# Relation coefficients moved ahead of the fourth softmax piece, with one float32 product per four slots

## The chip, the cores and the metric

The kernel runs on one core of one Trainium2 chip. The metric is the time of one execution in device microseconds. A profiled execution gives the trace, in which every instruction has a start and a duration. PE is TensorE (PEld its weight loads), DVE is VectorE, ACT is ScalarE, POOL is GpSimd and SP is SyncE.

## What is computed

Four layers over N = 3125 nodes with D = 256 features: a graph layer over 50,000 edges, a mixture of experts whose gates come from graph attention, a second graph layer with relations, and a last mixture of experts. The change concerns the seam of the second and the third:

```python
# attention scores: a softmax over the 32768 edges of each target, then
msg = h[src] * alpha[:, :, None]
agg = jax.ops.segment_sum(msg, dst, num_segments=M)
...
# third layer: each edge has one of 32 relations, mixed from 8 bases
weight = jnp.einsum('rb,bio->rio', w_comp, bases)
xw = jnp.einsum('ni,rio->nro', h, weight)
msg = xw[src, rel_type] * norm
out = jax.ops.segment_sum(msg, dst, num_segments=h.shape[0])
```

The kernel does not form `xw`. It uses `w_comp[rel_type] * norm`, eight coefficients for each edge: these are the relation coefficients, `coefs` (tile `slot_coefs`), of 128 partitions by KT = 592 slots by 8 bases. They depend only on the inputs.

## The kernel before

The function `attention_and_experts` writes the program of each engine by hand; the engines meet through semaphores, and each engine runs its own list in order.

*Experts.* Twenty units (4 experts by 5 chunks) run on TensorE as `up` (L1633) and `down` (L1646). ScalarE applies the gelu (L1529), VectorE adds a bias to the results (L1840), and SP stores them.

*Gathers.* Beside the units POOL gathers one row per attention edge into `gall`, 256 gathers of 128 edges (L1487), in 64 groups of four. Before each group it waits until a gather two groups back has landed, and for the progress of the experts that `experts_before(i)` names; groups 57 to 63 wait for the last unit's products only.

*Softmax pieces.* The edges lie in 256 columns that `CUT` divides into four pieces. `piece(c)` on VectorE waits until its columns have landed, scans for the running maximum (L1801), lets ScalarE take the exponents (`exponents`, L1520) and scans for the sums (L1820). The last piece, columns 224 to 256, comes after the last unit. ScalarE's queue stores its sums, and SP loads the rows of the experts' results (L1459) once the last sums are ready.

*Carry and ends.* The sums that run over from one partition to the next are worked out by VectorE, TensorE (L1657 to L1663) and ScalarE (L1538). POOL gathers the sums at the segments' ends, 25 gathers (L1495), and scatters the carry among them (L1494). L1895 on VectorE, which waits for the end gathers, starts the rest of the attention; TensorE combines the experts afterwards (L1692).

*Relation coefficients.* Between the carry and L1895 stands a loop of RS = 37 steps, 16 slots each. In a step VectorE compares the slots' relations with the 32 relations (`relations`, L1880, bf16 one-hots); TensorE turns four blocks of 128 by 128 (`turn_relations`, L1670); ScalarE copies them out of PSUM (L1543); TensorE multiplies each block, as the stationary operand, with the mixing weights of 32 columns (L1683); and VectorE multiplies with the edge's norm into `coefs` (L1891). One-hots, turned blocks and both PSUM banks are double buffered. The weights are float32. So that bf16 products give them in full, VectorE has split them into three bf16 parts (L1769, L1771), and each block is multiplied three times into the same sum.

`coefs` lies where the experts' second weights `W2` are, the one-hots in the first half of the experts' `W1`, and the turned blocks in the second. So the loop can't begin before the last unit.

Of the kernel before, what the change touches and what calls it, by code (L numbers as in the profile page):

```python
# [9 lines left out]
P = 128  # L10
# [1250 lines left out]
GATHERS = 4  # L1261
HALVES = [(kind, m) for m in range(-1, UNITS) for kind, m in (("up", m + 1), ("down", m)) if 0 <= m < UNITS]


def experts_before(i):
# [3 lines left out]
    if half >= len(HALVES):  # L1269
        return HALVES[-1][0], CT * UNITS  # L1270
# [8 lines left out]
def attention_and_experts(nc, common, a, X, iota, ident, att, drams, coefs, y_dram, xn_dram):  # L1279
# [3 lines left out]
    with ExitStack() as ctx:  # L1283
# [29 lines left out]
        relhot_t = [free.bitcast(BF16)[:, k * RQ // QT * P:(k + 1) * RQ // QT * P].rearrange("p (q e) -> p q e", e=P) for k in range(2)]  # L1313
        wparts = sb("wcomp_parts", [P, 3, QT * BASES], BF16)
# [19 lines left out]
        wrest = flags[:, :, :].rearrange("p n w -> p (n w)")[:, 0:QT * BASES]  # L1334
# [133 lines left out]
        def _(pool):  # L1468
# [12 lines left out]
            for i in range(GT // GATHERS):  # L1481
# [3 lines left out]
                pool.wait_ge(h_ready if kind == "up" else y_ready, items)  # L1485
# [12 lines left out]
        def _(act):  # L1498
# [24 lines left out]
            for m in range(UNITS):  # L1523
# [7 lines left out]
                for c in range(PIECES):  # L1531
                    if min(AFTER_UNIT[c] + 2, UNITS - 1) == m:
                        exponents(c)
            act.wait_ge(sums_ready, PIECES)
# [4 lines left out]
            for i in range(RS):  # L1539
                act.wait_ge(relt_ready, i + 1)  # L1540
                if i > 1:
                    act.wait_ge(coef_ready, i - 1)
                nc.scalar.activation(relhot_t[i % 2].rearrange("p q e -> p (q e)"), relt_ps[i % 2], ACT.Copy).then_inc(relt_copied, 1)  # L1543
# [32 lines left out]
        def _(pe):  # L1576
# [79 lines left out]
            pe.wait_ge(carry_steps, ENDS)  # L1656
            nc.tensor.matmul(lines_ps[:, 0, :], sums[:, GT - 1, 0:GW], att.after[:, :], start=True, stop=True)  # L1657
            nc.tensor.matmul(lines_ps[:, 1, :], last_top[:, :], att.after[:, :], start=True, stop=True)
            nc.tensor.matmul(lines_ps[:, 2, :], flags[:, 0, :], ident[:, :], start=True, stop=True)
            nc.tensor.matmul(lines_ps[:, 3, :], flags[:, 1, :], att.after[:, :], start=True, stop=True).then_inc(carry_replies, 1)  # L1660
            pe.wait_ge(carry_steps, RUN)
            nc.tensor.matmul(carry_ps[:, 0:GW], run[:, :], ident[0:GW, 0:GW], start=True, stop=True)
# [34 lines left out]
        def _(dve):  # L1697
# [70 lines left out]
            for n in range(3):  # L1768
                link(V.tensor_copy(wparts[:, n, :], left))  # L1769
                if n < 2:  # L1770
                    link(V.tensor_tensor(wrest, left, wparts[:, n, :], ALU.subtract))  # L1771
                    left = wrest
# [690 lines left out]
```

## Time and profile before

| | |
|---|---|
| runs | 2454.57, 2449.64, 2442.05 us, median 2449.64 |
| profiled execution | 2446.71 us, its span 2444.9 us |
| PE busy | 1714.3 us (70% of the span) |
| DVE busy | 1305.3 us (53%) |
| ACT busy | 701.2 us (29%) |
| POOL busy | 1070.8 us (44%) |
| mean granted TensorE clock | 0.829 |

An engine is busy while it runs an instruction; waits, and the issue of DMAs by SP and ScalarE, are not counted. The granted clock is the share of full speed that TensorE's clock had: 1.00 is 2.4 GHz and 0.50 is 1.2 GHz. In the rows below, [... <-X] is the idle time of the engine just before an instruction, and what ended it as far as the trace shows; "remote" is a semaphore event that it can't place, "issue" no wait that it shows. Times are counted from the start of the span. A group's form is partitions by elements, with the type.

### The profile page before, as it was taken

To read this page: it belongs to the slowest core of one execution; us is meant where nothing else is said; L and a number is where in the kernel's file an instruction comes from. 1 tells how busy PE (TensorE), PEld (TensorE's weight loads), DVE (VectorE), ACT (ScalarE), POOL (GpSimd) and SP (SyncE) were. 2 spreads that over 40 slices of the span, in tenths; PEclk is the share of its full clock that TensorE was granted. 3 is DMA by queue.
4 is the path that set the end of the run, shared out by engine and by line. 5 is a ranking of instruction groups with operands and counts; after the bars stand their busy time and mean duration, and the time that the engine had idled before them with its cause. 6 is when DMAs were issued, how large, how long until landed. Compare 5 with 4: busy or idle time off the path is not lost. (4 is left out here: it accounts for less than half of the span.)

```text
span 2444.9 us, 36227 instructions
## 1 busy us (share of the span) xinstructions
PE 1714.3 (70%) x8780; PEld 1361.2 (56%) x8781; DVE 1305.3 (53%) x3720; ACT 701.2 (29%) x1570; POOL 1070.8 (44%) x1102
## 2 busy tenths in 40 slices
PE   2775567677768999994163556566556667996998
PEld 1443345445446877783153545556545555885776
DVE  7876766677675213122275546556556665225335
ACT  0011255555523222220055322223222221001221
POOL 2676666565514666666402555545554550000000
PEclk9876687887889999997577776777877778998999
DMA  4223233333332232321415333333433332332001
GB/s 161 80 86 95 82 98 100 95 104 100 96 92 14 77 85 85 85 80 51 121 56 182 96 113 103 109 105 112 121 108 105 103 107 106 121 140 65 7 1 53
DMA packets 164850, 226.27 MB, mean 93 GB/s; under 512 B 35636, under 2 KB 123990, under 8 KB 161942
## 3 DMA queue, kind: packets, MB, share of 16 engines
q0 software_dynamic: 47392, 105.58, 15.8%
q1 hardware_dynamic: 114048, 115.99, 15.3%
q10 hardware_dynamic: 3318, 3.59, 0.4%
q8 instruction: 44, 0.72, 0.1%
q14 instruction: 48, 0.39, 0.1%
HBM read 172.48 MB, written 105.03 MB: 114 GB/s over the span
## 5 line engine op out<-in xcount | busy, mean ns | idle before, releaser
L2090 PE MATMUL part<-coef,held 128*128 128x128 f32 x2368 | 427.6, 348 | 309.9 <-DVE window_sums L2112 139.8
L2090 PEld LDWEIGHTS part<-coef,held 128*128 128x128 f32 x2368 | 385.8, 251 | 351.9 <-DVE window_sums L2112 188.7
L472 POOL DMA_INDIRECT edge_rows<-xn_table,edge_source x391 | 373.6, 956 | 429.2 <-ACT held L2078 212.1
L472 POOL DMA_INDIRECT shared_space<-xn_table,edge_source x391 | 399.8, 1023 | 284.2 <-issue 109.1
L2112 DVE SCALAR_TENSOR_TENSOR window_sums<-window_sums,fine_keep,part 128x256 f32 x592 | 284.2, 480 | 253.8 <-issue 175.6
L762 PE MATMUL part<-shared_space,hot 128*128 x832 | 303.7, 504 | 123.4 <-issue 64.1
L2078 ACT ACTIVATE held<-edge_rows 128x256 f32 x592 | 202.4, 405 | 498.9 <-remote 223.4
L1487 POOL DMA_INDIRECT gall<-attention_table,attention_source x256 | 245.1, 957 | 129.9 <-issue 69.5
L762 PEld LDWEIGHTS part<-shared_space,hot 128*128 128x128 f32 x832 | 180.8, 244 | 194.9 <-issue 172.7
L1147 DVE TENSOR_TENSOR shared_space<-shared_space,part 128x257 f32 x416 | 174.7, 420 | 139.4 <-remote 49.5
L2099 DVE SCALAR_TENSOR_TENSOR coef<-iota,fine_target,slot_coefs 128x128 f32<-128x128 f32 x592 | 205.6, 349 | 56.2 <-issue 39.6
L1633 PE MATMUL ps_of_attention<-shared_space,W 128*128 128x320 f32 x640 | 178.3, 436 | 4.8 <-issue 3.7
L1646 PE MATMUL ps_of_attention<-slot_coefs,hid 128*128 128x256 f32 x800 | 176.2, 379 | 5.2 <-DVE ys L1840 5.2
L1840 DVE TENSOR_TENSOR ys<-ps_of_attention,b 128x256 f32<-128x256 f32 x100 | 40.4, 422 | 255.6 <-PE ps_of_attention L1646 216.7
L1646 PEld LDWEIGHTS ps_of_attention<-slot_coefs,hid 128*128 128x128 f32 x800 | 151.8, 190 | 28.6 <-DVE ys L1840 3.8
L1633 PEld LDWEIGHTS ps_of_attention<-shared_space,W 128*128 128x128 f32 x640 | 121.5, 191 | 56.3 <-issue 6.2
L1529 ACT ACTIVATE hid<-ps_of_attention,b 128x320 f32<-128x320 f32 x160 | 82.4, 527 | 229.3 <-PE ps_of_attention L1633 183.6
L2259 PE MATMUL z_ps<-bases,z 128*128 128x256 f32 x672 | 147.7, 379 | 0.0
L2259 PEld LDWEIGHTS z_ps<-bases,z 128*128 128x128 f32 x672 | 126.5, 190 | 16.6
L661 ACT ACTIVATE sort_apart<-slot_iota,sort_col 128x256 bf16<-128x256 f32 x256 | 109.1, 496 | 40.4 <-DVEq L1088 29.4
L2283 PE MATMUL h_ps<-XNT,V 128*128 128x320 f32 x320 | 90.1, 441 | 13.7 <-DMA V<-in_L_ffn_W 13.7
L2295 PE MATMUL y_ps<-window_sums 128*128 128x256 f32 x400 | 88.1, 379 | 0.5 <-DVE XN L2425 0.5
(467 smaller groups left out, 1940.6 us busy)
## 6 DMA issues: line engine op xcount, KB each, us to landing
basis_sums<-window_sums SPq DMA_DIRECT2D x74, 1024.0 KB
z<-basis_sums SPq DMA_DIRECT2D x21, 1024.0 KB, 4.8
expert_rows<-ys SPq DMA_DIRECT2D x20, 640.0 KB
shared_space<-expert_rows SPq DMA_DIRECT2D x25, 512.0 KB, 4.8
W<-in_L_ffn_W SPq DMA_DIRECT2D x20, 512.0 KB
gall<-attention_digits SPq DMA_DIRECT2D x32, 256.0 KB
xn_table<-shared_space SPq DMA_DIRECT2D x10, 640.0 KB, 4.0
shared_space<-xn_table,edge_source POOLq DMA_INDIRECT x391
```

The source lines that it names most:

```text
L472: pool.indirect_dma_start(rows[:, b % ring, 0:D], None, table, bass.IndirectOffsetOnAxis(ap=esrc[:, b:b + 1].bitcast(U32), axis=0)).then_i ...
L661: nc.scalar.activation(apart[:, t, :], edges.slot_iota[:, 0:GT], ACT.Abs, bias=col[k][:, q * 4 + t:q * 4 + t + 1]).then_inc(apart_ready, 1)
L762: nc.tensor.matmul(part[:, n % BANKS, 0:D + 1], hot[n // HOT][:, n % HOT, :], rows[:, ds(at[n], 1), :].rearrange("p o d -> p (o d)"), star ...
L1147: V.tensor_tensor(to, to, part[:, n % BANKS, 0:D + 1], ALU.add).then_inc(added, 1)
L1487: pool.indirect_dma_start(gall[:, k, :], None, drams.table, at(att.source[:, k:k + 1])).then_inc(flights[i % FLIGHT], 16)
L1633: mm = nc.tensor.matmul(h_ps[:, n % BANKS_E, 0:HALF], W1[m % 2][:, c, f * P:(f + 1) * P], XNT[:, c, lo:lo + HALF], start=(c == 0), stop=(c ...
L1646: mm = nc.tensor.matmul(y_ps[:, (m * CT + t) % BANKS_E, :], hid[m % 2][:, f, t * P:(t + 1) * P], W2[:, m % EXPERTS, f, :], start=(f == 0), ...
L2078: nc.scalar.activation(held[j * STEP + n][:, :], rows[:, ds(at[n], 1), :].rearrange("p o d -> p (o d)"), ACT.Copy).then_inc(copied, 1)
L2090: mm = nc.tensor.matmul(part[n][:, c * P:(c + 1) * P], held[n][:, c * P:(c + 1) * P], coef[n][:, :, :].rearrange("p b w -> p (b w)"), star ...
L2099: V.scalar_tensor_tensor(coef[j * STEP + n][:, :, :], iota[:, 0:WIN].unsqueeze(1).to_broadcast([P, BASES, WIN]), fine.target[:, ds(i * STE ...
L2112: V.scalar_tensor_tensor(to, to, fine.keep[:, ds(i * STEP + n, 1)], part[j * STEP + n].rearrange("p (k w) -> p k w", w=WIN), ALU.mult, ALU ...
L2259: mm = nc.tensor.matmul(z_ps[:, m % 2, 0:D], of, bases[:, b, c, :], start=(n == 0), stop=(n == DC * BASES - 1))
```

## The change

Three things are changed. The whole loop of the relation coefficients is moved, on VectorE, TensorE and ScalarE, from behind the carry to between the third and the fourth softmax piece. The turned blocks are held as float32 instead of bf16, and each is multiplied once with the float32 weights `wcomp` in place of three times with bf16 parts; the parts and the instructions that make them are gone. And the last seven groups of POOL's gathers get other conditions: group 57 waits for the last unit's products as before, group 58 + n for 7 (n + 1) steps of the loop, and group 63 for all 37.

```diff
+GATED = 3 * 38 // 2
@@ def experts_before(i):
     half = halves + 2
     if half >= len(HALVES):
-        return HALVES[-1][0], CT * UNITS
+        return "coefs", 7 * (i - GATED)
@@ tiles
-        relhot_t = [free.bitcast(BF16)[:, k * RQ // QT * P:(k + 1) * RQ // QT * P].rearrange("p (q e) -> p q e", e=P) for k in range(2)]
-        wparts = sb("wcomp_parts", [P, 3, QT * BASES], BF16)
+        relhot_t = [free[:, k * RQ // QT * P:(k + 1) * RQ // QT * P].rearrange("p (q e) -> p q e", e=P) for k in range(2)]
@@ gpsimd
-                pool.wait_ge(h_ready if kind == "up" else y_ready, items)
+                if i == GATED:
+                    pool.wait_ge(y_ready, CT * UNITS)
+                elif kind == "coefs":
+                    pool.wait_ge(coefs_made, min(items, RS))
+                else:
+                    pool.wait_ge(h_ready if kind == "up" else y_ready, items)
@@ scalar, behind the last unit's gelus
-                for c in range(PIECES):
+                for c in range(PIECES - 1):
                     if min(AFTER_UNIT[c] + 2, UNITS - 1) == m:
                         exponents(c)
+            for i in range(RS):
+                act.wait_ge(relt_ready, i + 1)
+                if i > 1:
+                    act.wait_ge(coef_ready, i - 1)
+                nc.scalar.activation(relhot_t[i % 2].rearrange("p q e -> p (q e)"), relt_ps[i % 2], ACT.Copy).then_inc(relt_copied, 1)
+            exponents(PIECES - 1)
             act.wait_ge(sums_ready, PIECES)
...
             act.wait_ge(carry_steps, ROWS)
             nc.scalar.activation(factor[:, :, :], factor[:, :, :], ACT.Exp).then_inc(carry_replies, 1)
-            for i in range(RS):
...
@@ tensor, behind down(UNITS - 1) and ahead of the carry; turn_relations is the same
+            turn_relations(0)
+            for i in range(RS):
+                if i + 1 < RS:
+                    turn_relations(i + 1)
+                pe.wait_ge(relt_copied, i + 1)
+                if i > 1:
+                    pe.wait_ge(coefs_made, i - 1)
+                for q in range(RQ // QT):
+                    mm = nc.tensor.matmul(coef_ps[i % 2][:, q * QT * BASES:(q + 1) * QT * BASES], relhot_t[i % 2][:, q, :],
+                                          wcomp[:, :, :].rearrange("p q b -> p (q b)"), start=True, stop=True)
+                mm.then_inc(coef_ready, 1)
             pe.wait_ge(carry_steps, ENDS)
...
-                for q in range(RQ // QT):
-                    for n in range(3):
-                        mm = nc.tensor.matmul(coef_ps[i % 2][:, q * QT * BASES:(q + 1) * QT * BASES], relhot_t[i % 2][:, q, :],
-                                              wparts[:, n, :], start=(n == 0), stop=(n == 2))
-                mm.then_inc(coef_ready, 1)
@@ vector, ahead of the units
-            left = wcomp[:, :, :].rearrange("p q b -> p (q b)")
-            for n in range(3):
-                link(V.tensor_copy(wparts[:, n, :], left))
-                if n < 2:
-                    link(V.tensor_tensor(wrest, left, wparts[:, n, :], ALU.subtract))
-                    left = wrest
@@ vector, behind the last unit and the third piece
-                for c in range(PIECES):
+                for c in range(PIECES - 1):
                     if AFTER_UNIT[c] == m:
...
+            link(V.tensor_copy(relation, iota[:, 0:RELS].unsqueeze(2).to_broadcast([P, RELS, QT])))
+            relations(0)
+            relations(1)
+            for i in range(RS):
+                if i + 2 < RS:
+                    relations(i + 2)
+                dve.wait_ge(coef_ready, i + 1)
+                V.tensor_tensor(coefs[:, i * RQ:(i + 1) * RQ, :], coef_ps[i % 2].rearrange("p (t b) -> p t b", b=BASES),
+                                att.norm[:, i * RQ:(i + 1) * RQ].unsqueeze(2).to_broadcast([P, RQ, BASES]), ALU.mult).then_inc(coefs_made, 1)
+
+            for _ in piece(PIECES - 1):
                 pass
```

## Rows read from the trace of the kernel before

**Rows 1.** Busy time by stretch: length, engines (instructions), granted clock, DMA share, GB/s.

```profile
1138.00:1167.70 29.70, 0.00 (x0) 0.00 (x0) 0.12 (x1) 0.00 (x0) 22.63 (x24) 0.50 0.21 53
1185.90:1217.70 31.80, 3.39 (x52) 2.65 (x52) 2.61 (x8) 1.68 (x3) 21.47 (x23) 0.50 0.69 152
1217.70:1224.40 6.70, 5.78 (x105) 4.82 (x106) 4.25 (x15) 4.08 (x8) 0.00 (x0) 0.51 0.01 2
1224.40:1245.50 21.10, 19.66 (x440) 15.72 (x438) 16.62 (x55) 16.11 (x27) 0.00 (x0) 1.00 0.02 3
```

**Rows 2.** Timeline, 1137 to 1170 us: start, duration, engine, instruction, idle before.

```profile
1137.03 1.09 DVE L1820 TENSOR_TENSOR_SCAN shared_space<-shared_space,gall 128x56 f32<-128x56 f32 x4
...
1166.70 0.94 POOL L1487 DMA_INDIRECT gall<-attention_table,attention_source  x1 [0.30 <-issue]
1169.14 0.41 DVE L1797 TENSOR_TENSOR shared_space<-gall,shared_space 128x128 f32<-128x128 f32 x1 [31.02 <-issue]
```

**Rows 3.** Timeline of the relation loop, 1186 to 1246 us.

```profile
1188.69 0.53 PE L1683 MATMUL ps_of_attention<-wcomp_parts,W 128*128 128x32 bf16 x12
...
1213.13 0.94 POOL L1495 DMA_INDIRECT hid<-edge_sums,segment_end  x1 [0.30 <-issue]
1217.12 0.29 DVE L1891 TENSOR_TENSOR slot_coefs<-ps_of_attention,slot_norm 128x128 f32<-128x128 f32 x1 [24.02 <-remote]
...
1219.57 0.59 PE L1670 MATMUL ps_of_attention<-identb,W 128*128 128x128 bf16 x4
...
1219.95 0.53 PE L1683 MATMUL ps_of_attention<-wcomp_parts,W 128*128 128x32 bf16 x12
...
1227.73 0.40 PE L1670 MATMUL ps_of_attention<-identb,W 128*128 128x128 bf16 x4
...
1227.97 0.47 PE L1683 MATMUL ps_of_attention<-wcomp_parts,W 128*128 128x32 bf16 x12
...
1245.42 0.25 DVE L1895 TENSOR_TENSOR hid<-hid,self_arg 128x100 f32<-128x100 f32 x1
```

**Rows 4.** Expert units: timeline, and POOL's gathers from 849.3 to 859.2.

```profile
1109.42 8.79 PE L1646 MATMUL ps_of_attention<-slot_coefs,hid 128*128 128x256 f32 x40
...
1115.90 0.94 POOL L1487 DMA_INDIRECT gall<-attention_table,attention_source  x1 [0.30 <-issue]
1119.42 1.42 DVE L1840 TENSOR_TENSOR ys<-ps_of_attention,b 128x256 f32<-128x256 f32 x4 [3.77 <-PE ps_of_attention L1646]
...
856.83 0.42 DVE L1840 TENSOR_TENSOR ys<-ps_of_attention,b 128x256 f32<-128x256 f32 x1 [1.30 <-issue]
...
L1487 POOL DMA_INDIRECT gall<-attention_table,attention_source x8 | 7.5, 943 | 4.2 <-issue 2.1 <-PE ps_of_attention L1633 2.1
```

**Rows 5.** Timeline of VectorE where the scans of the targets begin.

```profile
797.38 0.62 DVE L1776 TENSOR_REDUCE some_start<-shared_space 128x1 f32<-128x256 f32 x1 [18.37 <-DMA first_value<-attention_targets,first_target]
```

**Rows 6.** Groups by line and form, 1224.4 to 1245.5 us: busy, mean ns, idle.

```profile
L1543 ACT ACTIVATE W<-ps_of_attention 128x512 bf16<-128x512 bf16 x27 | 16.1, 597 | 4.3 <-PE ps_of_attention L1670 3.8
...
L1880 DVE TENSOR_TENSOR W<-slot_relb,W 128x512 bf16<-128x512 bf16 x26 | 10.8, 415 | 0.0
```

**Rows 7.** Early float32 products of two columns: timeline, and durations (min/median/max).

```profile
42.39 1.02 PE L711 MATMUL equal_ps<-block_slots,before 128*128 128x2 f32 x4 [16.80 <-DVEq L907]
...
45.40 1.42 PE L713 MATMUL equal_ps<-block_slots,ones 128*128 128x2 f32 x6
...
L713 PEld LDWEIGHTS equal_ps<-block_slots,ones x12: 333/333/333, 43.2 to 46.4; 128*128 128x128 f32 x12
```

**Rows 8.** Float32 products where the granted clock is 1.00.

```profile
742.26 0.52 PE L1606 MATMUL ps_of_attention<-wgat,shared_space 128*128 128x16 f32 x4
742.62 0.42 PE L1581 MATMUL ps_of_attention<-ident,shared_space 128*128 128x128 f32 x2
...
1370.45 9.19 PE L2090 MATMUL part<-coef,held 128*128 128x128 f32 x63 [1.76 <-issue]
...
L876 PEld LDWEIGHTS few_ps<-ones,shared_space x4: 190/192/192, 684.5 to 684.9; 128*128 128x128 f32 x4
```

More of the change, by code:

```diff
@@ L1333, in attention_and_experts @@
         flags = sb("carry_flags", [P, 2, GW])
-        wrest = flags[:, :, :].rearrange("p n w -> p (n w)")[:, 0:QT * BASES]
         last_top = sb("last_top", [P, GW])
@@ L1538, in _ @@
             nc.scalar.activation(factor[:, :, :], factor[:, :, :], ACT.Exp).then_inc(carry_replies, 1)
-            for i in range(RS):
[L1540 to L1543, printed above, removed]
             act.wait_ge(arg_ready, 1)
@@ L1654, in _ @@
             down(UNITS - 1)
[L1656 to L1662, printed above, removed]
-            nc.tensor.matmul(carry_ps[:, GW:EW], peak[:, 1:P + 1], ident[0:GW, C16:GW], start=True, stop=True).then_inc(carry_replies, 1)
             def turn_relations(i):
@@ L1681, in _ @@
                 for q in range(RQ // QT):
-                    for n in range(3):
-                        mm = nc.tensor.matmul(coef_ps[i % 2][:, q * QT * BASES:(q + 1) * QT * BASES], relhot_t[i % 2][:, q, :],
-                                              wparts[:, n, :], start=(n == 0), stop=(n == 2))
+                    mm = nc.tensor.matmul(coef_ps[i % 2][:, q * QT * BASES:(q + 1) * QT * BASES], relhot_t[i % 2][:, q, :],
+                                          wcomp[:, :, :].rearrange("p q b -> p (q b)"), start=True, stop=True)
                 mm.then_inc(coef_ready, 1)
+            pe.wait_ge(carry_steps, ENDS)
+            nc.tensor.matmul(lines_ps[:, 0, :], sums[:, GT - 1, 0:GW], att.after[:, :], start=True, stop=True)
+            nc.tensor.matmul(lines_ps[:, 1, :], last_top[:, :], att.after[:, :], start=True, stop=True)
+            nc.tensor.matmul(lines_ps[:, 2, :], flags[:, 0, :], ident[:, :], start=True, stop=True)
+            nc.tensor.matmul(lines_ps[:, 3, :], flags[:, 1, :], att.after[:, :], start=True, stop=True).then_inc(carry_replies, 1)
+            pe.wait_ge(carry_steps, RUN)
+            nc.tensor.matmul(carry_ps[:, 0:GW], run[:, :], ident[0:GW, 0:GW], start=True, stop=True)
+            nc.tensor.matmul(carry_ps[:, GW:EW], peak[:, 1:P + 1], ident[0:GW, C16:GW], start=True, stop=True).then_inc(carry_replies, 1)
             for t in range(NT):
@@ L1848, in _, with relations @@
             for _ in parts:
+                pass
+            def relations(i):
+                if i > 1:
+                    dve.wait_ge(relt_ready, i - 1)
+                V.tensor_tensor(relhot[i % 2], relb[:, i * RQ:(i + 1) * RQ].rearrange("p (g q) -> p g q", q=QT).unsqueeze(2)
+                                .to_broadcast([P, RQ // QT, RELS, QT]), relation.unsqueeze(1).to_broadcast([P, RQ // QT, RELS, QT]),
+                                ALU.is_equal).then_inc(relhot_ready, 1)
+            link(V.tensor_copy(relation, iota[:, 0:RELS].unsqueeze(2).to_broadcast([P, RELS, QT])))
[8 more added lines that the diff above has]
+            for _ in piece(PIECES - 1):
                 pass
```

15 lines of the change are left out of this document (removed).

## The prediction

> **What bounds the kernel now.** I read the busy time by stretch first, because TensorE at 70% of the span says nothing of one stage. Between 1138.0 and 1167.7 us TensorE and ScalarE run nothing and VectorE almost nothing, while POOL gathers; between 1185.9 and 1217.7 all three compute engines are nearly idle again [rows 1]. The timeline says what each hole waits for. VectorE finishes the third softmax piece at 1138.12 (1137.03 + 1.09) and waits for the last gather, which ends on POOL at 1167.64 (1166.70 + 0.94); the fourth piece starts at 1169.14. Its sums are stored [rows 2], POOL begins the end-of-segment gathers, and the carry is worked out beside them. From then on VectorE has only the relation coefficients until the segment ends are in. The last end gather finishes on POOL at 1214.07 (1213.13 + 0.94); VectorE resumes at 1217.12, and the relations end with L1895 at 1245.42 [rows 3]. L1895 waits for the end gathers too, but at 1245.42 they are long in: the relations are what is late. So the end of this stage is set by POOL up to about 1217, then by the relation loop for 28.3 us (1245.42 - 1217.12).
>
> Why the loop stood still in between: the product that the eviction at 1217.12 waits for is recorded at 1188.69 [rows 3]. The same shows in the expert units: five tiles of products run from 1109.42 to 1118.21, and VectorE takes four of them only at 1119.42, after the gathers that ran through them have ended at 1116.84; between 849.3 and 859.2, with 8 gathers, the evictions keep TensorE's pace, 1.30 idle and 0.42 busy [rows 4]. TensorE's signals are held while a long unbroken run of gathers lasts. Whether this holds here costs nothing before the change, since the end gathers need the same time.
>
> **What the change removes.** The relations leave the path behind the carry, and what is next there is the landing of the end gathers. That is bounded from below by 1214.07 + 1.5 (the delay between the last expert-stage gather and VectorE, 1169.14 - 1167.64) = 1215.6 and from above by 1217.12, when VectorE was released. Nothing else in L1895's waits is later: the one load besides follows the carry scatter. The gain is 28.3 to 29.8 us; I take 28.3, as the held signals end when the gathers have landed. The five small VectorE instructions that made the split weights go as well; they lie ahead of a wait of 18.37 us for the first targets, which hides them: I count 0, and without that cover five of the smallest steps would be about 1 us [rows 5].
>
> **What it adds.** The relations stand between the third and fourth piece, and the last seven groups of four gathers are gated: one group per seven coefficient steps, the last behind all 37. The cost is how much later than 1169.14 the fourth piece starts. That depends on one number, the time T of a step.
>
> ScalarE's copy (0.60, the same 512 elements out of PSUM with the wider output) bounds T from below, VectorE's compare (0.42) and the multiply lie beside it; the old loop runs 27 copies in 21.1 us, 0.78 each [rows 1, 6]. TensorE's part is four transposes and the products. There are now four float32 products in place of twelve bf16 ones, and a float32 product is two records in this trace (the bases and the heads are issued so). Hence eight records a step.
> At the lower clock (granted 0.50): transposes 1219.95 - 1219.57 = 0.38 [rows 3]; float32 records with hardly any moving column, six in 1.42 us of which the last load takes 0.33: (1.42 - 0.33) / 5 = 0.217 each [rows 7]; 8 x 0.217 = 1.74. T = 2.12.
> At the full clock: transposes 1227.97 - 1227.73 = 0.24 [rows 3]; float32 records 0.09 each (742.26 to 742.62, four, 16 columns) to 0.146 (9.19 us for 63, 128 columns) [rows 8]. I take 0.11, nearer to the narrow row: T = 0.24 + 0.88 = 1.12, between 0.96 and 1.41.
> In both cases TensorE is the engine that bounds the loop, which it is not today; the other two hide beside it.
>
> Which clock? At 1138 it is 0.50, TensorE being idle. In the old loop, it stayed there for 6.7 us of nearly unbroken bf16 work (1217.7 to 1224.4) and then rose to 1.00 [rows 1]. The new loop is different work, with products that spend nearly all their time loading float32 weights. The nearest row is the early stretch of float32 products of two columns, issued from 42.39 to 46.82 us; from 43.2 on all loads of its longer line take 333 ns, the duration of the lower clock; at the full one such a load takes some 190 [rows 7, 8]. I take the lower clock for the whole loop. This is the choice on which the sign hangs.
>
> Sum at T = 2.12: VectorE needs 0.8 us after 1138.12 for the first one-hots, so TensorE starts at 1138.9. Step 35 (which releases the last but one group) is done at 1138.9 + 35 x 2.12 + 1.0 (first copy and last eviction) = 1214.1. Then two groups of four gathers, 4 x 1.25 us each (0.94 and the gap of 0.30) with 0.1 to start, and 1.5 to VectorE: 1214.1 + 10.1 + 1.5 = 1225.7. The other groups hide beside the loop (5 us in every 14.8), and the old wait of 31 us for gathers is inside this time. The fourth piece is 1225.7 - 1169.1 = 56.6 us later. Everything behind it moves as it is: piece, its store on ScalarE's queue, the row loads on SP's queue behind the same signal (they end well ahead of the combination), the carry on TensorE and the end gathers on POOL. Exponents of the fourth piece now queue on ScalarE behind 37 copies and the TensorE carry products behind the relations, but both need the fourth piece anyway. Net: 56.6 - 28.3 = +28.3. On the profiled execution, 2446.71 (its span is 2444.9): 2475.0. The median of the runs shown is 2449.64, 2.9 higher: 2477.9. I predict 2478. The own range of this case: the gain 1.5 better, 0.2 us of T either way (7 us): 2469 to 2486.
>
> In general the fourth piece starts at 1151.5 + 35 T, and the change breaks even where that is 1197.4 (1169.1 + 28.3), so at T = 1.31.
>
> **Rivals.**
> *The clock rises early.* For: the old loop did rise, and the new one leaves TensorE hardly a gap. Against: rows 7. Time: 6.7 us of warming take 3.2 steps instead of 6, 3.2 us lost; 1151.5 + 35 x 1.12 + 3.2 = 1193.9, 24.8 later; 24.8 - 28.3 = -3.5: 2446. With T between 0.96 and 1.41: 2440 to 2456. No change that can be told. Beside it stands the Trainium skill, TensorE: Matmul & The Clock Gate, What's actually happening, by which the clock follows how busy the engine has been recently and activity releases it; read plainly, the loop is busy without a gap and would get the full clock, so 2446. This trace agrees for the bf16 loop and does not show it for 4.4 us of narrow float32 products.
> *The clock comes and goes*, as it does around TensorE's pauses elsewhere: T between the two, 2452 to 2468, slower.
> *The gathers hold the signals of the loop too.* For: 24 us of it in the old loop. Against: a gated group is four gathers, and 8 in a run held nothing. Price: up to 6.5 us (5.0 and the landing) for each of five groups, 32 us at most: 2486 to 2510.
> *Faster (the other side): TensorE does not bound the loop.* If a narrow float32 record could be issued about as fast as the bf16 ones, the loop would keep its 0.76, and the fourth piece would start at 1151.5 + 26.6 = 1178.1, 9 us later; 2449.6 + 9.0 - 28.3 = 2430. It decides for faster by over 0.5% (12.2 us) below T = 0.96 without any warming. Against: no float32 row here is under 0.09, and the clock at the start is 0.50.
>
> **Numbers.** Half clock throughout 0.63, coming and going 0.11, held signals 0.05: slower by over 0.5% (about what a measurement of this kernel can tell from no change) 0.76, as 0.03 of the second lies inside the bound. Early full clock 0.16 and those 0.03: same 0.19. Faster 0.05. The range must reach from the early clock to the upper end of the first case and a little into the held one: 2446 to 2490.
>
> **What would show it.** Right: the new product line with eight records a step, loads of 333 ns and granted clock 0.50 from 1138 to about 1216; steps 2.1 us apart; POOL idle between groups of four; the fourth piece near 1226; L1895 about 48 us behind it with no relation work between. Wrong: loads of 190 ns after a few us, steps of 1.1 us. Wrong in another way: waits of VectorE on the products that end when a group of gathers lands, or L1895 later than 48 us behind the piece, which would mean that the relations had covered something that is late by itself.

## The result, and the profile after

The changed kernel takes 2474.64 us (median of 4 runs, 2464.74 to 2476.25), the kernel before 2445.85 (4 runs, 2441.95 to 2454.57). The ratio is 1.0113, with a 95% interval of 1.0093 to 1.0133: 1.1% slower, 28.8 us. Predicted were 2478 and slower.

The profiled execution of the changed kernel took 2476.25 us, its span 2474.5, with a mean granted clock of 0.819. First the busy time by stretch (columns as in [rows 1]):

```profile
1147.10:1177.00 29.90, 28.82 (x168) 28.56 (x168) 9.52 (x30) 8.70 (x15) 3.78 (x4) 0.50 0.12 44
1177.00:1215.00 38.00, 38.00 (x221) 38.00 (x220) 11.21 (x36) 10.89 (x19) 11.35 (x12) 0.50 0.03 4
...
1246.00:1281.80 35.80, 1.01 (x4) 0.92 (x4) 2.30 (x8) 0.41 (x1) 24.80 (x26) 0.50 0.73 176
```

These lines answer to [rows 1]. Where TensorE did nothing for 30 us, it is now busy for 38.00 us out of 38.00, at a granted clock of 0.50. Behind the fourth piece the loop is gone: 1.01 us of TensorE while the end gathers run. What fills TensorE in the loop is seen in the groups of the stretch from 1177 to 1215 us (busy us, mean ns of one, idle before):

```profile
L1678 PE MATMUL ps_of_attention<-wcomp,W 128*128 128x32 f32 x149 | 34.8, 397 | 0.0
L1678 PEld LDWEIGHTS ps_of_attention<-wcomp,W 128*128 128x128 f32 x148 | 33.9, 333 | 0.0
...
L1542 ACT ACTIVATE W<-ps_of_attention 128x512 f32<-128x512 bf16 x19 | 11.3, 597 | 28.2 <-PE ps_of_attention L1666 23.7 <-PE ps_of_attention L1678 4.4
```

The loads of the float32 products take 333 ns each and 33.9 us of 38, at the duration of the lower clock [rows 7]. ScalarE's copy costs the 597 ns of before [rows 6], and is idle for 27.1 us of the stretch (it is busy for 10.9). The timeline shows the order of the seam, and answers to [rows 2, 3]:

```profile
1145.94 1.09 DVE L1818 TENSOR_TENSOR_SCAN shared_space<-shared_space,gall 128x56 f32<-128x56 f32 x4
...
1151.17 0.29 DVE L1863 TENSOR_TENSOR slot_coefs<-ps_of_attention,slot_norm 128x128 f32<-128x128 f32 x1 [2.17 <-PE ps_of_attention L1678]
...
1153.25 0.29 DVE L1863 TENSOR_TENSOR slot_coefs<-ps_of_attention,slot_norm 128x128 f32<-128x128 f32 x1 [1.46 <-PE ps_of_attention L1678]
...
1164.21 0.94 POOL L1491 DMA_INDIRECT gall<-attention_table,attention_source  x1 [17.68 <-DVE slot_coefs L1863]
...
1178.77 0.95 POOL L1491 DMA_INDIRECT gall<-attention_table,attention_source  x1 [9.86 <-DVE slot_coefs L1863]
...
1225.67 0.29 DVE L1863 TENSOR_TENSOR slot_coefs<-ps_of_attention,slot_norm 128x128 f32<-128x128 f32 x1 [1.42 <-PE ps_of_attention L1678]
...
1231.20 0.95 POOL L1491 DMA_INDIRECT gall<-attention_table,attention_source  x1 [0.30 <-issue]
1233.49 0.42 DVE L1795 TENSOR_TENSOR shared_space<-gall,shared_space 128x128 f32<-128x128 f32 x1 [7.53 <-POOLq L1478]
...
1277.48 0.95 POOL L1499 DMA_INDIRECT hid<-edge_sums,segment_end  x1 [0.31 <-issue]
1281.80 0.26 DVE L1896 TENSOR_TENSOR hid<-hid,self_arg 128x100 f32<-128x100 f32 x1 [31.66 <-DMA hid<-edge_sums,segment_end]
```

The third piece ends at 1147.03 (1145.94 + 1.09). The evictions come every 2.08 us, each behind a wait of 1.46 us for the products of L1678, and POOL's groups of four wait for them (17.68 us, 9.86 us). The last group ends at 1232.15 and the fourth piece starts at 1233.49. The end gathers finish on POOL at 1278.43, and L1896 (L1895 before) starts at 1281.80, after a wait that ends with the landing of an end gather and not with relation work.

I compare executions by two lengths: **A**, from the end of the third piece to the start of the fourth, and **B**, from there to the instruction that takes in the segment ends. Before: A = 1169.14 - 1138.12 = 31.02 and B = 1245.42 - 1169.14 = 76.28 [rows 2, 3]. After: A = 86.46, B = 48.31. So A grew by 55.4 and B shrank by 28.0: +27.5 in the part that the change touches, against 28.8 measured. The two profiled executions also differ elsewhere: the third piece ends 8.9 us later after the change, and what lies behind L1896 is 6.8 us shorter (2474.5 - 1281.80 = 1192.7 against 2444.9 - 1245.42 = 1199.5). This nearly cancels. It looks like a difference between executions: experiments 3 and 4 have the changed kernel's code ahead of their own edits, which lie behind the last expert unit, and end their third piece at 1138.02 and 1132.81; in setting Y below, both kernels end it within 0.03 us of each other.

### The profile page after: what moved, and what is told of

Same layout as the page of the kernel before. It is cut to its first block and busy times, and to the rows that moved or that the text cites. A ratio compares the mean times of both kernels' runs of the same rounds, so it can differ in the third digit from the quotient of the medians.

```text
span 2474.5 us, 35926 instructions
## 1 busy us (share of the span) xinstructions
PE 1772.0 (72%) x8632; PEld 1422.6 (57%) x8633; DVE 1307.0 (53%) x3715; ACT 701.4 (28%) x1570; POOL 1071.8 (43%) x1102
## 5 line engine op out<-in xcount | busy, mean ns | idle before, releaser
L2091 PE MATMUL part<-coef,held 128*128 128x128 f32 x2368 | 432.6, 352 | 299.1 <-DVE window_sums L2113 124.9
L2091 PEld LDWEIGHTS part<-coef,held 128*128 128x128 f32 x2368 | 391.6, 255 | 340.3 <-DVE window_sums L2113 184.3
L1838 DVE TENSOR_TENSOR ys<-ps_of_attention,b 128x256 f32<-128x256 f32 x100 | 42.1, 424 | 257.6 <-PE ps_of_attention L1651 198.2
```

The source lines that it names most:

```text
L2091: mm = nc.tensor.matmul(part[n][:, c * P:(c + 1) * P], held[n][:, c * P:(c + 1) * P], coef[n][:, :, :].rearrange("p b w -> p (b w)"), star ...
```

## The experiments

The kernel before took 2444 us beside experiments 1 to 4, 2098 to 2099 beside 5 to 11, and 2413 beside 12. I call these three settings X, Y and Z; X's times are those of the result. My expectations take them for three chips. That is an inference, and the record does not bear it out: it lists chip 1 for experiments 1 to 4, 11 for 5 to 10, 1 again for 11, and 2 for 12, so the number 1 stands beside times of X and of Y. Whether that is one chip in two conditions or two chips with one number, it does not say. Ratios are always to the kernel before in the same setting. The traces by A and B, in us:

| | setting | length A | length B | A + B, against before | measured, us (ratio, 95% interval) |
|---|---|---|---|---|---|
| before | X | 31.02 | 76.28 | | |
| after | X | 86.46 | 48.31 | +27.5 | +28.8 (1.0113, 1.0093 to 1.0133) |
| 1: bf16 products | X | 58.10 | 48.58 | -0.6 | +0.6 (0.9999, 0.9983 to 1.0015) |
| 2: float32, old place | X | 31.04 | 118.35 | +42.1 | +39.2 (1.016, 1.0138 to 1.0182) |
| 3: no gates | X | 103.56 | 48.70 | +45.0 | +41.5 (1.0171, 1.0144 to 1.0198) |
| 4: warm start | X | 84.07 | 49.07 | +25.8 | +15.9 (1.0075, 1.0047 to 1.0103) |
| 9: before again | Y | 30.90 | 50.03 | | |
| 8: after again | Y | 86.46 | 48.64 | +54.2 | +53.6 (1.026, 1.0245 to 1.0276) |
| 5: bf16, ones in 2 steps | Y | 40.10 | 48.54 | +7.7 | +8.4 (1.0044, 1.0028 to 1.0059) |
| 6: bf16, ones in 1.6 steps | Y | 36.43 | 48.41 | +3.9 | +3.6 (1.0016, 1.0007 to 1.0025) |
| 7: warm start and fill | Y | 66.54 | 48.43 | +34.0 | +32.5 (1.0158, 1.0142 to 1.0173) |
| 12: bf16 products | Z | 57.63 | 48.61 | | +0.1 (0.9994, 0.9973 to 1.0015) |

**1. The move alone.** The changed kernel, with the three bf16 products, the bf16 turned blocks and the split weights of before.

```diff
...
-                    mm = nc.tensor.matmul(coef_ps[i % 2][:, q * QT * BASES:(q + 1) * QT * BASES], relhot_t[i % 2][:, q, :],
-                                          wcomp[:, :, :].rearrange("p q b -> p (q b)"), start=True, stop=True)
+                    for n in range(3):
+                        mm = nc.tensor.matmul(coef_ps[i % 2][:, q * QT * BASES:(q + 1) * QT * BASES], relhot_t[i % 2][:, q, :],
+                                              wparts[:, n, :], start=(n == 0), stop=(n == 2))
...
```

> The changed kernel with the move and the gates, but with the old three bf16 products. My theory (the loss is all in the float32 products at half clock): steps of about 0.80 us, the granted clock rises to 1.00 some 7 us into the loop, the fourth piece starts 17 us before break-even, about 2429 us (ratio to before 0.993). Rival (the place beside the gathers is itself costly, because TensorE's signals are held while gathers run): with 7 steps in 5.6 us and 5.0 us of gathers per group the runs of gathers become nearly unbroken, each group costs up to 5 us, 2435 to 2455 us.

Measured: 2444.86 us, no difference (ratio 0.9999). My number, 2429, is missed by 16 us. The timeline of the profiled execution, from just before a group of gathers:

```profile
1176.62 0.29 DVE L1872 TENSOR_TENSOR slot_coefs<-ps_of_attention,slot_norm 128x128 f32<-128x128 f32 x1
...
1177.18 0.94 POOL L1493 DMA_INDIRECT gall<-attention_table,attention_source  x1 [5.01 <-DVE slot_coefs L1872]
...
1177.49 0.29 DVE L1872 TENSOR_TENSOR slot_coefs<-ps_of_attention,slot_norm 128x128 f32<-128x128 f32 x1 [0.25 <-PE ps_of_attention L1681]
...
1177.83 0.51 PE L1681 MATMUL ps_of_attention<-wcomp_parts,W 128*128 128x32 bf16 x12
...
1178.60 0.51 PE L1681 MATMUL ps_of_attention<-wcomp_parts,W 128*128 128x32 bf16 x12
...
1180.03 0.29 DVE L1872 TENSOR_TENSOR slot_coefs<-ps_of_attention,slot_norm 128x128 f32<-128x128 f32 x1 [1.91 <-PE ps_of_attention L1681]
...
1182.99 0.29 DVE L1872 TENSOR_TENSOR slot_coefs<-ps_of_attention,slot_norm 128x128 f32<-128x128 f32 x1 [2.34 <-PE ps_of_attention L1681]
...
1183.53 0.28 DVE L1872 TENSOR_TENSOR slot_coefs<-ps_of_attention,slot_norm 128x128 f32<-128x128 f32 x1
...
1198.12 0.42 DVE L1804 TENSOR_TENSOR shared_space<-gall,shared_space 128x128 f32<-128x128 f32 x1 [8.87 <-issue]
```

Steps are 0.8 us apart until a group of four gathers begins at 1177.18. The products that start at 1177.83 end at 1178.34 and are evicted at 1180.03, 1.69 us later; those of 1178.60 end at 1179.11 and are evicted at 1182.99, 3.88 us later. VectorE sat idle for it, 1.91 and 2.34 us. The pattern is the same in each of the four groups inside the loop, and lengthens the mean step to (1189.0 - 1142.7) / 36 = 1.286 us. So the rival is right: groups of four do hold TensorE's signals in this loop. The rise of the clock that my theory counted on came only in part: the granted clock of this loop is 0.65 on the mean (1142 to 1189 us) and 0.50 from 1173 us on. That costs little: with the clock at 0.50, from 1184.64 to 1187.16, the steps are 0.84 us, and experiment 6's at 1.00 are 0.77. The move by itself is worth nothing in setting X, and the whole loss is that of the float32 product.

**2. The product alone.** The kernel before, with one float32 product in place of the three bf16 ones; nothing is moved and nothing is gated.

```diff
...
-                    for n in range(3):
-                        mm = nc.tensor.matmul(coef_ps[i % 2][:, q * QT * BASES:(q + 1) * QT * BASES], relhot_t[i % 2][:, q, :],
-                                              wparts[:, n, :], start=(n == 0), stop=(n == 2))
+                    mm = nc.tensor.matmul(coef_ps[i % 2][:, q * QT * BASES:(q + 1) * QT * BASES], relhot_t[i % 2][:, q, :],
+                                          wcomp[:, :, :].rearrange("p q b -> p (q b)"), start=True, stop=True)
...
```

> The kernel before with the float32 product alone, loop in its old place. My theory: the loop stands still beside the end gathers as before and then needs 35 steps of 2.08 us instead of 0.80: 45 us more, about 2491 us (ratio 1.018), clock 0.50 through the whole loop. Rival (the clock rises after some microseconds as it does with bf16): steps of 1.12 us, 12 us more, 2458 us.

Measured: 2483.44 us, +39.2; my number was 2491, the rival's 2458. The timeline on VectorE around the end of the end gathers:

```profile
1199.79 0.29 DVE L1882 TENSOR_TENSOR slot_coefs<-ps_of_attention,slot_norm 128x128 f32<-128x128 f32 x1 [5.09 <-issue]
...
1220.14 0.29 DVE L1882 TENSOR_TENSOR slot_coefs<-ps_of_attention,slot_norm 128x128 f32<-128x128 f32 x1 [19.73 <-remote]
...
1224.88 0.29 DVE L1882 TENSOR_TENSOR slot_coefs<-ps_of_attention,slot_norm 128x128 f32<-128x128 f32 x1 [1.88 <-PE ps_of_attention L1680]
```

The loop stands still beside the end gathers as in [rows 3] (19.73 us of wait at 1220.14) and then needs 71 us, to 1291.1, for what took the kernel before 28.3 [rows 3]. The granted clock is 0.50 in all of it, with TensorE busy for 68.07 of 68.50 us. So the slow step does not come from the new place or from the gathers: it comes with the product.

**3. No gates.** The changed kernel, its last seven groups waiting for the last unit's products only, as in the kernel before.

```diff
                 elif kind == "coefs":
-                    pool.wait_ge(coefs_made, min(items, RS))
+                    pool.wait_ge(y_ready, CT * UNITS)
```

> The changed kernel without the gates: all 28 last gathers run on in one stretch of 35 us beside the first half of the loop. My theory (an unbroken run of more than about six gathers holds TensorE's signals): the loop nearly stands still from its start until the gathers have landed, some 29 us, then needs its 2.08 us a step; the fourth piece starts at once behind it. Some 20 us later than with the gates: about 2495 us. Rival (gathers and loop do not disturb each other): the loop keeps 2.08 us from the start and the last two groups' 7 us are saved: about 2468 us.

Measured: 2485.77 us, +41.5, which is 12.7 more than with gates; between my 2495 and the rival's 2468, nearer to mine. The timeline:

```profile
1151.15 0.29 DVE L1863 TENSOR_TENSOR slot_coefs<-ps_of_attention,slot_norm 128x128 f32<-128x128 f32 x1 [8.38 <-remote]
...
1166.62 0.94 POOL L1491 DMA_INDIRECT gall<-attention_table,attention_source  x1 [0.30 <-issue]
1172.20 0.29 DVE L1863 TENSOR_TENSOR slot_coefs<-ps_of_attention,slot_norm 128x128 f32<-128x128 f32 x1 [20.43 <-remote]
...
1177.26 0.29 DVE L1863 TENSOR_TENSOR slot_coefs<-ps_of_attention,slot_norm 128x128 f32<-128x128 f32 x1 [1.46 <-PE ps_of_attention L1678]
```

With 28 gathers in one run the second eviction comes after a wait of 8.38 us and the third after one of 20.43 us, 4.6 us after the last gather ended at 1167.56. Behind that the steps are 2.08 us apart. The gates thus do earn 17.1 us of length A (103.56 - 86.46); the one thing they change is that the gathers come in short runs.

**4. A warm start.** The changed kernel with 30 bf16 products of 512 columns ahead of the loop; their results are not used.

```diff
+            for _ in range(30):
+                nc.tensor.matmul(ps[:, 3, :], identb[:, :], relb[:, 0:512], start=True, stop=True)
             turn_relations(0)
```

> The changed kernel with 30 further bf16 products of 512 columns (results unused) on TensorE between the last expert unit and the loop, where it would be idle, so that it enters the loop at full clock. If the loop can keep the full clock once it has it: steps of about 1.12 us instead of 2.08, 34 us less than the changed kernel, about 2441 us. If the loop can't keep it: the clock falls back to 0.50 within a few microseconds of the loop's start and the time is within 4 us of the changed kernel, 2470 to 2475 us. I lean to the second, 0.55 to 0.45.

Measured: 2460.11 us. By the lengths A and B it is 1.6 us better than the changed kernel; the rest of its 14.5 us is no work of this experiment: most of it lies ahead of the seam, where the third piece of its profiled execution ended at 1132.81 and the code is that of the changed kernel. Its trace answers the question of the clock. Windows, then the timeline:

```profile
1120.00:1133.70 13.70, 10.24 (x46) 5.62 (x45) 12.43 (x41) 0.58 (x1) 7.92 (x8) 1.00 0.16 35
1133.70:1137.60 3.90, 3.54 (x38) 3.27 (x37) 1.94 (x6) 2.07 (x4) 0.00 (x0) 0.96 0.61 244
1137.60:1209.00 71.40, 71.33 (x409) 71.20 (x408) 20.57 (x68) 19.91 (x34) 17.73 (x19) 0.50 0.04 4
```

```profile
1135.90 0.29 DVE L1865 TENSOR_TENSOR slot_coefs<-ps_of_attention,slot_norm 128x128 f32<-128x128 f32 x1 [1.34 <-PE ps_of_attention L1680]
1135.93 1.03 PE L1680 MATMUL ps_of_attention<-wcomp,W 128*128 128x32 f32 x8
...
1136.99 0.29 DVE L1865 TENSOR_TENSOR slot_coefs<-ps_of_attention,slot_norm 128x128 f32<-128x128 f32 x1 [0.47 <-PE ps_of_attention L1680]
...
1138.62 0.29 DVE L1865 TENSOR_TENSOR slot_coefs<-ps_of_attention,slot_norm 128x128 f32<-128x128 f32 x1 [1.01 <-PE ps_of_attention L1680]
...
1138.81 1.86 PE L1680 MATMUL ps_of_attention<-wcomp,W 128*128 128x32 f32 x8
...
1140.70 0.29 DVE L1865 TENSOR_TENSOR slot_coefs<-ps_of_attention,slot_norm 128x128 f32<-128x128 f32 x1 [1.46 <-PE ps_of_attention L1680]
```

The loop begins at the full clock. Two steps are 1.09 us apart (1135.90 to 1136.99), then one of 1.63, then 2.08. The granted clock fell to 0.50 while TensorE had been busy for 3.54 of 3.90 us with loads and products, and stayed there for 71.33 busy us out of 71.40. It was not idleness that took it.

**5 and 6. Single gathers between the steps.** The kernel of experiment 1, with each of the 24 gated gathers let go by itself, one for every two steps (experiment 5) and one for every 1.6 steps (experiment 6, shown; 5 has `* 2 // 1` where 6 has `* 8 // 5`).

```diff
                 elif kind == "coefs":
-                    pool.wait_ge(coefs_made, min(items, RS))
+                    pass
...
                 for k in range(i * GATHERS, (i + 1) * GATHERS):
+                    if i > GATED:
+                        pool.wait_ge(coefs_made, min((k - GATHERS * (GATED + 1) + 1) * 8 // 5, RS))
```

> The changed kernel with the old three bf16 products, and the 24 gated gathers let go one at a time, one for every two steps, instead of in fours for seven steps. In the bf16 loop in its new place (first experiment) a step takes 0.86 us on the mean, but each group of four gathers made two steps of 2.6 and 2.9 us. Theory (the signals of TensorE are held back by the length of an unbroken run of gathers, counted in TensorE instructions: the late signals come 32 to 44 products into a run): with pauses of about 0.8 us between the gathers no step is long, the loop takes 37 x 0.86 = 32 us, six gathers are left behind it, the fourth piece starts 43 us behind the end of the third (58.1 in the first experiment), 2430 us. Rival (each gather costs the loop its 0.9 us wherever it is): the fourth piece stays at 55 to 60 us, 2443 to 2447.

> As the one before, but one gather for every 1.6 steps, so that only the last gathers wait for the end of the loop. The pause between two gathers is then about 0.44 us where 0.30 is what POOL leaves between two gathers by itself. Theory, if such a pause is enough to release the signals: steps of 0.86 us, the fourth piece 36.5 us behind the end of the third, 2423 us. If the pause is too short, the run counts as unbroken, steps of 2.6 us and more come back within it, and the fourth piece starts 45 to 60 us behind: 2432 to 2447.

These ran in setting Y, where the kernel before takes 2098.47 us. They take 2106.89 and 2102.09, both slower than before there. In times they can't be held against the expectations, which were for setting X. By length A they can: 40.10 and 36.43, where the theory said 43 and 36.5. But this does not test the theory, for two reasons. In this setting no signal was late even beside unbroken gathers (experiment 9). And the steps are (1057.6 - 1030.0) / 36 = 0.77 us in experiment 6, not 0.86, so the pauses that were to release the signals hardly exist: of the 23 between its 24 gathers, 21 are the 0.30 us that POOL leaves by itself. What sets its length A is POOL and not the loop. The timeline of experiment 6, with POOL hardly pausing:

```profile
1039.85 1.05 POOL L1495 DMA_INDIRECT gall<-attention_table,attention_source  x1 [0.30 <-DVE slot_coefs L1874]
1040.08 0.29 DVE L1874 TENSOR_TENSOR slot_coefs<-ps_of_attention,slot_norm 128x128 f32<-128x128 f32 x1
...
1040.91 0.29 DVE L1874 TENSOR_TENSOR slot_coefs<-ps_of_attention,slot_norm 128x128 f32<-128x128 f32 x1 [0.21 <-PE ps_of_attention L1683]
...
1041.20 1.16 POOL L1495 DMA_INDIRECT gall<-attention_table,attention_source  x1 [0.30 <-DVE slot_coefs L1874]
...
1041.72 0.29 DVE L1874 TENSOR_TENSOR slot_coefs<-ps_of_attention,slot_norm 128x128 f32<-128x128 f32 x1 [0.18 <-PE ps_of_attention L1683]
```

In these lines an eviction follows within 0.21 us of idle time, gather or not; of all 37, only the first and the last two wait for longer than 0.28 us (0.76, 0.54 and 0.52). Experiments 10 and 11 are the kernel of experiment 6 again, in the hope of setting X:

> The sixth experiment's kernel (three bf16 products, one gather for every 1.6 steps) again, to have it on a chip on which TensorE's signals are held. There: if single gathers with a pause of some 0.4 us release the signals, the fourth piece starts 36.5 us behind the end of the third (58.1 with groups of four) and the time is 22 us below that of the kernel before, 2423 beside 2445; if such pauses count as none, steps of 2.6 us and more come back, the fourth piece starts 45 to 60 us behind and the time is 2432 to 2447. On the other kind of chip: as before, 36.4 us and 3 to 4 us above the kernel before.

> The kernel of the sixth and tenth experiments once more, for the case that it now runs on a chip that holds TensorE's signals (the kernel before at 2445 us there). There: if pauses of some 0.4 us release the signals, the fourth piece starts 36.5 us behind the end of the third and the time is 2423; if not, 45 to 60 us behind, 2432 to 2447. On the other chip again: 36.4 us, 0.2% above the kernel before.

Both ran in setting Y again: 2102.26 (ratio 1.0017, 1.0008 to 1.0026) and 2102.28 (1.0014, 1.0004 to 1.0024), A = 36.48 and 36.40. The number repeats; the question for setting X stays open.

**7. Wide products among the narrow ones.** The warm start, and in each step two bf16 products of 512 columns behind the float32 ones; their results are not used. The diff shows what comes on top of experiment 4.

```diff
...
                                           wcomp[:, :, :].rearrange("p q b -> p (q b)"), start=True, stop=True)
+                for _ in range(2):
+                    nc.tensor.matmul(ps[:, 5, :], identb[:, :], relb[:, 0:512], start=True, stop=True)
                 mm.then_inc(coef_ready, 1)
```

> The changed kernel with the warm start of the fourth experiment (30 bf16 products of 512 columns ahead of the loop) and two more such products behind the four float32 ones of every step; their results are not used. In the fourth experiment the granted clock was 1.00 as the loop began and fell to 0.50 2.7 us into it, though TensorE never paused. Theory (the clock is lost because float32 products of 32 columns move few columns for the time they take, not because of pauses): with 1024 more columns a step the clock stays at 1.00, T = 1.12 + 2 x 0.216 = 1.55, the fourth piece about 1.55 x 35 + 13 = 67 us behind the end of the third (86.5 in the changed kernel), 2456. Rival (float32 products lower the clock whatever runs beside them, or the fall was a matter of this place in time): T = 2.08 + 0.86 = 2.94, the fourth piece 116 us behind, 2505.

Measured, in setting Y: 2130.94 us, where the changed kernel takes 2152.07. With more work in each step it is 21 us faster; the warm start alone gave 1.6 us in setting X. The windows:

```profile
1032.00:1060.00 28.00, 27.74 (x257) 23.74 (x260) 11.66 (x37) 11.00 (x19) 7.96 (x8) 1.00 0.03 5
1060.00:1086.00 26.00, 25.79 (x237) 22.07 (x240) 10.05 (x32) 9.89 (x17) 9.66 (x10) 1.00 0.03 5
```

The granted clock is 1.00 from end to end, and the steps are (1086.2 - 1031.7) / 36 = 1.51 us apart, 1.55 expected and 2.94 by the rival. A = 66.54, 67 expected. TensorE is busy without a gap in this loop and in that of the changed kernel; this one holds wide products too. The warm start without the wide products was not run in setting Y. Experiment 8 shows that without both the loop runs at 0.50 there throughout; that the clock would fall there after a warm start alone, as it did in X, is not shown. Which property of the wide products keeps it was not taken apart either.

**8. The changed kernel again.**

> The changed kernel once more. Its profiled execution reached the end of the third piece 8.9 us later than the kernel before did (1147.0 against 1138.1), ahead of all that the change touches, and three of its four times were near 2475, one 2464.7. If that lateness belongs to single executions, some of these times are near 2465 and the median lies between 2464 and 2475; if it belongs to this program, all are near 2475. By the stage that the change touches alone it should be 2445 + 27.5 = 2472.

It ran in setting Y as well: 2152.07 us, +53.6, nearly twice the loss in setting X. Length A is the same to the hundredth, 86.46, and the third piece ends at 1027.11, where it ends at 1027.08 in the kernel before. What differs is what the move gains: length B falls from 50.03 to 48.64, by 1.4 us and not by 28.

**9. The kernel before again,** for its trace in setting Y.

> The kernel before, once more, for its trace. The fifth to eighth experiments ran on another chip, on which the kernel before took 2098.5 us where it took 2445 on the first one, and the changed kernel 2152. On that chip TensorE's signals were never late beside gathers. On a chip of that kind I expect the relation loop of the kernel before to run beside the end gathers at 0.8 us a step and to end before they have landed, so that the move gains 3 us at most there; time near 2098. On a chip of the first kind: the loop stands still from its second step to the end of the end gathers, L1895 is 28 us behind their landing, time 2440 to 2452.

Measured 2097.86 us. The evictions of its loop at the start and at the end, the last end gather, and L1895:

```profile
1077.35 0.29 DVE L1891 TENSOR_TENSOR slot_coefs<-ps_of_attention,slot_norm 128x128 f32<-128x128 f32 x1 [0.77 <-PE ps_of_attention L1683]
...
1078.10 0.29 DVE L1891 TENSOR_TENSOR slot_coefs<-ps_of_attention,slot_norm 128x128 f32<-128x128 f32 x1
...
1079.00 0.29 DVE L1891 TENSOR_TENSOR slot_coefs<-ps_of_attention,slot_norm 128x128 f32<-128x128 f32 x1 [0.28 <-PE ps_of_attention L1683]
...
1103.07 1.20 POOL L1495 DMA_INDIRECT hid<-edge_sums,segment_end  x1 [0.30 <-issue]
...
1105.64 0.29 DVE L1891 TENSOR_TENSOR slot_coefs<-ps_of_attention,slot_norm 128x128 f32<-128x128 f32 x1 [0.25 <-PE ps_of_attention L1683]
1108.01 0.26 DVE L1895 TENSOR_TENSOR hid<-hid,self_arg 128x100 f32<-128x100 f32 x1 [2.08 <-DMA hid<-edge_sums,segment_end]
```

The loop runs beside the end gathers at 0.79 us a step ((1105.6 - 1077.3) / 36) and ends at 1105.93; the last gather ends on POOL at 1104.27, and L1895 waits 2.08 us for the landing. So the loop is off the path here, as this experiment's expectation says. The relations still cost the kernel before about 1.4 us: beside them POOL takes 33.7 us from the first end gather to the last (1070.61 to 1104.27), and 32.3 in experiment 8, where they are gone.

**12. The move alone, again.**

> The first experiment's kernel (the changed kernel with the old three bf16 products) again. On the chip of the fifth to eleventh experiments, whose signals were never late: steps of 0.78 us with no long ones beside the groups of four, step 35 done at 2.7 + 35 x 0.78 + 0.3 = 30.3 us behind the end of the third piece, two groups of gathers and the landing 11.6 more, so the fourth piece 41.9 us behind (58.1 on the first chip), against 30.9 in the kernel before; with 1.9 gained behind it 2098 + 11.0 - 1.9 = 2107. On the first chip: 2445 again.

This one ran in a third setting, Z, with the kernel before at 2412.99 us: 2413.11, ratio 0.9994 (0.9973 to 1.0015). Its trace is like that of setting X: steps of some 2.5 and 2.9 us beside each of the four groups of four in the loop, and a length A of 57.63. So two settings of three show the held signals, and in both the move alone neither gains nor loses.

## Why the prediction was right, step by step

*The lower clock for the whole loop, from the row of the narrow early products [rows 7].* Right: 0.50 from 1147.1 to 1226 us. It was the choice on which the sign hung, and it was in part luck. The row held 4.4 us of such work. The bf16 loop stayed at 0.50 for 6.7 us before it rose [rows 1], so the row could not tell a loop that stays low from one that rises a little later. And the prediction does not say that the profile lists a granted clock of 1.00 for that stretch:

```profile
42.80:46.90 4.10, 4.02 (x19) 3.94 (x19) 2.64 (x15) 0.00 (x0) 0.61 (x1) 1.00 0.51 174
```

It went by the loads of 333 ns instead. The later traces bear that out: the same kind of load takes 333 ns at a granted 0.50 in the changed kernel and 192 at 1.00 in experiment 7. The clock entries of this trace begin only at 56.96 us, so the 1.00 is no measurement.

Experiments 4 and 7 show what the loop does with the clock: these products lose the full clock even when they are given it (setting X), and TensorE keeps it when wide ones stand among them (setting Y). The rule of the Trainium skill that stood beside the rival (TensorE: Matmul & The Clock Gate, What's actually happening), read plainly as busy time, does not hold for this loop; 71.33 busy us out of 71.40 got 0.50.

*T = 0.38 + 8 x 0.217 = 2.12.* It was 2.08. The eight float32 records are 0.213 each between starts (1.70), and the transposes 0.38. At full clock 1.12 was said; experiment 4's first steps are 1.09, and experiment 7's 1.51 less two wide products of 0.216 is 1.08.

*A = 13.4 + 35 T (1151.5 - 1138.1, and 35 steps).* It gives 86.2 for T = 2.08, where 86.46 was seen; 58.4 for experiment 1 (58.10) and 66.3 for experiment 7 (66.54). The fourth piece came 55.4 us later against the third, and 56.6 was said: the 0.04 us of T times 35.

*The gain of 28.3, to the landing of the end gathers.* It was 28.0 in setting X: nothing was hidden behind the relations. What ends the wait is the landing, as said. L1896 stands 48.3 us behind the piece; 48 was said.

*Net +28.3, 2478 us.* By the lengths +27.5, by the runs +28.8. (The narrower range given with it, 1.5 and 7 us about 2478, is 2469.5 to 2485, not 2469 to 2486.) The 3.4 us between prediction and result are nearly the difference (3.8) of the medians of the kernel before, 2449.64 in the runs shown and 2445.85 with one more.

*The break-even at T = 1.31.* Experiment 1 sits on it: T = 1.29, net -0.6.

*"8 in a run held nothing", as the argument against held signals.* Right for this kernel, wrong as a reason. In the float32 loop no signal was late beside a group of four, but in the bf16 loop the same group of four cost two steps of 2.5 to 3 us (experiments 1 and 12). Nor was it true of all runs of eight: beside the one from 937.39 us in the kernel before, an eviction came after 3.15 us of idle time that the trace puts down to "remote". The number of gathers in a run does not decide. So the rival on the faster side was priced wrongly too: a loop at 0.76 a step would not have given 2430 in setting X, but 2445.

*The gain rests on signals that are held.* The prediction said so, but did not ask whether this always happens. In setting Y it does not, and there the same edit costs 53.6 us. In setting X the loss is softened by a gain that is only the removal of that stall. The changed kernel was not run in Z. That the total came out near the forecast thus also rests on the result having been measured in the setting of the trace that was read.

No kernel of these beats the kernel before. Experiment 6's may do so in setting X, by up to 22 us (a length A of 36.4 in place of 58.1 at a net of -0.6), if single gathers with short pauses let the signals through; that was expected and not measured.

## What to carry to other kernels

Three bf16 products that hide beside ScalarE are cheaper than one float32 product whose time is the loading of its weights: count the loads, and take their duration at the clock that such narrow work gets, from the nearest row of the same kind. Before a loop is moved next to a run of GpSimd gathers, ask whether its steps progress there at all, since length A was 58 us in the settings that held the signals and 36 in the one that did not (there with single gathers, so that two things differ). A small gain that rests on a stall which does not show in every setting should be taken from traces of more than one.

## What the runs showed of the hardware that was not expected

*The same kernel differs by 14% between settings, and held signals go with it.* The kernel before took 2445, 2413 and 2098 us. In Y no wait of the trace's list is put down to "remote"; in X the list of the changed kernel has this line among others (total us, times, longest):

```profile
ACT held L2079 <- remote: 193.0, 37, 10.4
```

The part behind the segment ends, gathers again with narrow stages between the engines, takes 1192.7 us in X and 2148.9 - 1162.21 = 986.7 in Y in the changed kernel. Busy times are alike where nothing waits (steps of the float32 loop 2.08 in both). That the held signals make up the difference is an inference from this; it was not taken apart. Nor is it known whether a setting is a chip: the record's chip number 1 stands beside times of X and of Y.

*When the signals are late.* Counted in the traces, from the first gather of a run: beside the four groups of four inside the bf16 loop, in X and Z, the first late signal is that of the 16th to 20th TensorE instruction (transposes and products, loads not counted), 1.6 to 1.9 us late, and that of the next products is 3.8 to 4.1 late. (Experiment 5's expectation put them 32 to 44 products into a run.) The unbroken runs beside the float32 loop fit this: in experiment 3 the 16th is on time, the 20th 1.6 us late and the 28th 7.0; in experiment 2 these are 0.4, 1.4 and 4.0 us late. But beside the groups of four in the changed kernel the 18th and the 22nd are on time every time. In Y all evictions of experiment 9 are on time, over 540 instructions into one run of 25 gathers and a scatter. The count alone does not decide, and what does is open: the loops differ also in how densely TensorE issues.

*A clock that falls while TensorE works.* In experiment 4 it fell from 1.00 to 0.50 with TensorE busy for 3.54 of 3.90 us, and in experiment 7 a warm start and the addition of 0.43 us of wide products to each step shortened the step from 2.08 to 1.51 us.
